# A transposing transfer in place of TensorE transposes in the dot-attention layer of a four-layer graph stack

## The chip, the cores and the metric
The kernel runs on one core of a Trainium2 chip. The metric is the device time of one execution in microseconds (us). Engines are called by the names of the profile: PE (TensorE matmul), PEld (TensorE weight load), DVE (VectorE), ACT (ScalarE), POOL (GpSimd) and SP (SyncE, which here only issues DMAs; SPq is its queue).

## The reference
The input x has shape 16 x 1024 x 64 (16 graphs of 1024 nodes with 64 channels), adj is a 1024 x 1024 mask. Four layers follow one another, each `x = x + layer(relu(layernorm(x)))`. Layers 0 and 3 are additive graph attention, layer 1 is a softmax per channel. The change touches layer 2, which is dot attention:

```
h = jnp.einsum('bnc,hdc->bhnd', x, Wh)            # 4 heads of 64
scores = jnp.einsum('...nd,...md->...nm', h, h)   # masked, softmax over m
out_h = jnp.einsum('...nm,...md->...nd', attn, h) + b
z = leaky_relu(cat(out_h)); h2 = z @ Wo.T         # 256 -> 64
out2 = attention of h2 with itself, as above; then leaky_relu and layernorm
```

So for each graph there are five attentions of 1024 x 1024 scores: four heads, and one over the projected heads, called the out unit.

## The kernel before
**Units.** Layer 2 is a list `UNITS` of 80 units, run one after the other: for each graph b head 0, head 1, the out unit of graph b - 1, head 2, head 3 (the first graph has no out unit between, and the last out unit comes later, inside layer 3). Every engine has its own program with this order written out by hand; semaphores join them.

**A tile.** A unit has T = 8 tiles of 128 rows. Tile jt has these steps: `dots` (PE, L1819: 8 matmuls with 512 columns into one of two score buffers S), the exponential from S to one of eight buffers of `ring` (ACT, L1066), the multiplication by the mask (DVE, L1412, `masked_weights`), and `dot_sums` (PE, L1638: 32 matmuls of 65 columns into ACC). PE issues `dots` of tile m and then `dot_sums` of tile m - LAG, with LAG = 3.

**Features.** The scores need the unit's features with the 64 channels on partitions, as a high fp16 part and the rest, also fp16 ("hi" and "lo"), stacked in FA: FA[:, par, 0] holds hi on partitions 0 to 63 and lo on 64 to 127, FA[:, par, 1] the two swapped. FA has two buffers (par), so features of the next unit are made beside the present one. They are made in this order, with the tile of the present unit in which each step stands in the program of its engine:
- tile 0: PE `values` (L1862), the projection by Wh or Wo, into both banks of AX, 64 columns for each of 8 node tiles; ACT `values` copies it to `v_pairs` (L1086) and squares it (L1087);
- tile 1: DVE `norms` (L1437, L1439) for the bound that the exponential subtracts;
- tile 2: PE `features` (L1871), four 128x128 fp32 transposes of `v_pairs` into AX bank 1; ACT copies the sums of the unit before (L877), then makes hi (L1100); DVE `epilogue` of the unit before (L1420, L1421);
- tile 3: DVE `feature_rest` makes lo (L1429); PE `spread_bound` (L1628); DVE `bias` (L1445) follows in tile 4;
- SP issues four DMAs of 64 KB after hi and four after lo (L513, L514, L519, L520). The first `dots` of the next unit waits for all eight (`features_in`).

POOL adds the bias to the values (L797), which gives V, the right side of `dot_sums`.

**Beside it.** In head 0 and head 3, PE turns two finished heads for the projection by Wo (`turn_heads`, L1839, 8 transposes, both banks of AX); ACT copies them to z_t (L1107). In head 3 this stands in tile 5 on PE and tile 6 on ACT; in head 0 in tile 6. In head 2, PE turns the normalized x of the next graph (`turn_norm`). The banks of AX are handed out by a table (`AX_AT`, filled by `place`), and each user waits until the last one freed its bank; DVE's `bias` frees bank 0.

Of the kernel before, what the change touches and what calls it, by code (L numbers as in the profile page):

```python
# [11 lines left out]
P = 128  # L12
# [18 lines left out]
def gnn_stack(nc, x, adj, w_gat0, w_gat0_t, a_gat0, w0, b0, wa, ba, wh_t, bh, wo_t, bo, gamma, beta,  # L31
# [11 lines left out]
    with ExitStack() as ctx:  # L43
# [79 lines left out]
        hi = sb("hi", [P, 2, HALF], F16)  # L123
        lo = sb("lo", [P, 2, HALF], F16)
        sq = sb("sq", [P, TD])
        v_by_pair = sb("v_pairs", [P, TD])
        v_pairs = v_by_pair[:, :].rearrange("p (q h d) -> p h q d", q=T // 2, h=2)
# [145 lines left out]
        lo_made = sem("lo_made")  # L273
        features_in = [sem("features_in0"), sem("features_in1")]
# [69 lines left out]

        def moved_by(u):

            return 16 * 8 * (u["n"] // 2 + 1)
# [53 lines left out]
        def place_values(u):  # L401

            for half in range(2):
                place(("V", u["n"], half), half)

        def place_features(u):

            place(("F", u["n"]), 1)
# [13 lines left out]
        place_features(UNITS[0])  # L422
        place_bound(UNITS[0])
        for u in UNITS[:-1]:
            if after(u):
                place_values(after(u))
                place_features(after(u))
                place_bound(after(u))
# [20 lines left out]
        place_features(LAST)  # L449
# [45 lines left out]
        def _(sp):  # L495
# [10 lines left out]
            for u in UNITS:  # L506
                par = buf_of(u)
                moved = features_in[par]
                sp.wait_ge(hi_made, u["n"] + 1)
                for half in range(2):  # L510
                    cols_of = slice(half * HALF, (half + 1) * HALF)
                    own = slice(half * D, (half + 1) * D)
                    sp.dma_start(FA[0:D, par, 0, cols_of], hi[own, par, :]).then_inc(moved, 16)  # L513
                    sp.dma_start(FA[D:P, par, 1, cols_of], hi[own, par, :]).then_inc(moved, 16)  # L514
                sp.wait_ge(lo_made, u["n"] + 1)
                for half in range(2):
                    cols_of = slice(half * HALF, (half + 1) * HALF)
                    own = slice(half * D, (half + 1) * D)
                    sp.dma_start(FA[D:P, par, 0, cols_of], lo[own, par, :]).then_inc(moved, 16)  # L519
                    sp.dma_start(FA[0:D, par, 1, cols_of], lo[own, par, :]).then_inc(moved, 16)  # L520
# [9 lines left out]
        def _(pool):  # L530
# [329 lines left out]
        def _(act):  # L860
# [219 lines left out]
            def values(u):  # L1080

                for half in range(2):
                    k, at = AX_AT["V", u["n"], half]
                    act.wait_ge(ax_full[k], at + 1)
                wait(act, v_made, u["n"])
# [5 lines left out]
                for k in range(2):  # L1091
                    act.sem_inc(ax_free[k], 1)

            def features(u):

                k, at = AX_AT["F", u["n"]]
                act.wait_ge(ax_full[k], at + 1)
                if u["n"] >= 2:
                    act.wait_ge(features_in[buf_of(u)], moved_by(UNITS[u["n"] - 2]))
                act.activation(hi[:, buf_of(u), :], AX[k][:, :], ACT.Copy).then_inc(hi_made, 1)  # L1100
# [12 lines left out]
            def dot_unit(u, jt):  # L1113
# [11 lines left out]
                if jt == 6 and is_head(u, 3):  # L1125
# [55 lines left out]
        def _(dve):  # L1181
# [242 lines left out]
            def feature_rest(u):  # L1424

                k, at = AX_AT["F", u["n"]]
# [3 lines left out]
                dve.wait_ge(lo_made, u["n"] + 1)  # L1430
                dve.sem_inc(ax_free[k], 1)
# [60 lines left out]
            def features(u):  # L1492
                norms(u)
                feature_rest(u)
# [12 lines left out]
            def last_layer():  # L1507
# [13 lines left out]
                for jt in range(T):  # L1521
# [56 lines left out]
        def _(pe):  # L1578
# [159 lines left out]
            def last_layer():  # L1738
# [12 lines left out]
                for jt in range(T):  # L1751
# [5 lines left out]
                    if jt == 2:  # L1757
                        features(LAST)
# [83 lines left out]
            def values(u):  # L1842
                n, out_unit = u["n"], u["kind"] == "out"
                if out_unit:
# [5 lines left out]
                chunks = range(2 if out_unit else 1)  # L1850
                for half in range(2):
                    take_bank(AX_AT["V", n, half])
                for t in range(T // 2):
                    for half in range(2):
                        for i in chunks:
                            for c in range(2):
# [3 lines left out]
                                else:  # L1860
                                    rows, w = node_tiles(u["b"], t, half, c), wh[half * D:(half + 1) * D, u["h"], :]
                                last = pe.matmul(AX[half][c * CUT:(c + 1) * CUT, t * D:(t + 1) * D], rows, w,  # L1862
# [99 lines left out]
```

## Time and profile before

| | |
|---|---|
| median of 3 runs | 1996.86 us (1995.81 to 1998.15) |
| the profiled execution | 1996.86 us, span 1995.1 us |
| PE busy | 1904.9 us (95%) |
| DVE busy | 1623.2 us (81%) |
| ACT busy | 1243.6 us (62%) |
| POOL busy | 1013.7 us (51%) |
| units of layer 2 (80) | about 408 us to 1785 us of the span, one more about 1815 us |

A unit begins with its first row of L1819 in the timeline of PE, and the projection (L1862) stands one tile behind that start. The projection tells which unit it is: `AX<-wo,z_t` stands in head 1 (the next unit is the out unit), `AX<-wh,h_t` in the others.

### The profile page before, as it was taken

What the parts mean: (1) busy time and instruction counts of PE and PEld (TensorE: products, weight loads), DVE (VectorE), ACT (ScalarE), POOL (GpSimd) and SP (SyncE); (2) the same over time, 40 slices, a digit from 0 to 9 for tenths busy, and PEclk for the clock granted to TensorE, in tenths of its full rate; (3) what the DMA queues carried; (4) which work ended last, traced back from release to release, by engine and by line L of the source; (5) the groups of instructions that cost most, each with busy time, mean ns of one, the idle gap of its engine ahead of it and who ended that gap; (6) DMA issues with size and microseconds to landing.
All of it is one profiled execution on the core that took longest, in us unless ns stands there. A gap on an engine that the chain in (4) does not pass through costs nothing.

```text
span 1995.1 us, 95063 instructions
## 1 busy us (share of the span) xinstructions
PE 1904.9 (95%) x43624; PEld 1563.2 (78%) x43624; DVE 1623.2 (81%) x1975; ACT 1243.6 (62%) x1886; POOL 1013.7 (51%) x742
## 2 busy tenths in 40 slices
PE   8998899999999999999999999999999999989998
PEld 6787799977777777777777777777777777767887
DVE  6999999567787878778787878788778877767998
ACT  5887676246666666666666666666666666654342
POOL 6676899432345444444544444553445454253653
PEclk7999999999999999999999999999999999999999
DMA  7000000011111111111111111111111111101111
GB/s 182 4 4 4 3 2 3 2 34 35 35 34 34 32 33 33 30 35 34 35 35 32 35 28 35 33 34 35 34 34 29 34 31 33 35 13 25 25 25 35
DMA packets 88255, 61.24 MB, mean 31 GB/s; under 512 B 45616, under 2 KB 86832, under 8 KB 87856
## 3 DMA queue, kind: packets, MB, share of 16 engines
q1 hardware_dynamic: 85632, 54.57, 11.2%
q8 instruction: 343, 5.62, 1.2%
q10 hardware_dynamic: 2224, 0.59, 0.1%
q14 instruction: 56, 0.46, 0.1%
HBM read 8.98 MB, written 4.19 MB: 7 GB/s over the span
## 4 chain that ended last, share of the span: by engine, by line
PE 69%; DVE 15%; ACT 5%; POOL 5%; issue 2%; DMA 2%; SPq 1%; ACTq 0%; POOLq 0%; DVEq 0%
PE ACC L1638 29%; PE S L1819 22%; PE S L1798 8%; DVE ring L1412 6%; PE AX L1862 3%; DVE ring L1266 2%; PE AX L1871 2%; PE AX L1839 2%; POOL sp_log L788 1%; POOL ln_sq L791 1%; DMA FA<-lo 1%; ACT ring L1066 1%; PE AX L1618 1%; DVE score L1421 1%; PE S L1695 1%
## 5 line engine op out<-in xcount | busy, mean ns | idle before, releaser
L1638 PEld LDWEIGHTS ACC<-V,ring 128*64 128x64 f32 x28672 | 953.5, 138 | 180.5 <-DVE ring L1266 34.0
L1412 DVE TENSOR_TENSOR ring<-ring,mask_self_t 128x1024 f32<-128x1024 f32 x640 | 822.1, 1287 | 270.0 <-ACT ring L1066 261.3
L1638 PE MATMUL ACC<-V,ring 128*64 128x65 f32 x28672 | 972.6, 223 | 29.7 <-DVE ring L1266 12.3
L1066 ACT ACTIVATE ring<-S,dot_bias 128x1024 f32<-128x1024 f32 x640 | 713.4, 1115 | 420.3 <-PE S L1819 384.4
L1819 PE MATMUL S<-FA 128*64 128x512 f16 x5120 | 666.5, 382 | 7.5 <-DMA FA<-lo 7.5
L1819 PEld LDWEIGHTS S<-FA 128*64 128x64 f16 x5120 | 253.3, 110 | 168.6 <-ACT ring L1066 15.9
L1266 DVE SCALAR_TENSOR_TENSOR ring<-S,pair_q,mask_t 128x1024 f32<-128x1024 f32 x256 | 315.1, 1272 | 15.1 <-DVE f_max L1278 4.6
L804 POOL TENSOR_TENSOR EV_both<-score,recip 128x512 f32<-128x512 f32 x64 | 115.4, 1803 | 222.3 <-DVE score L1421 222.2
L797 POOL TENSOR_TENSOR V<-v_pairs,bh_bc 128x512 f32<-128x512 f32 x64 | 95.4, 1490 | 164.9 <-ACT v_pairs L1086 164.9
L1798 PE MATMUL S<-parts,mask_t 128*128 128x128 bf16 x3072 | 172.0, 219 | 1.6 <-DVE o L1401 1.4
L1798 PEld LDWEIGHTS S<-parts,mask_t 128*128 128x128 bf16 x3072 | 171.6, 98 | 1.8 <-issue 1.8
L877 ACT ACTIVATE accs<-ACC 128x520 f32<-128x520 f32 x112 | 66.7, 596 | 95.3 <-PE ACC L1638 95.3
L600 POOL TENSOR_TENSOR ln_rstd<-ln_ve,neg_half 128x8 f32<-128x8 f32 x16 | 39.8, 2490 | 87.3 <-DVE ln_ve L1257 87.3
L1086 ACT ACTIVATE v_pairs<-AX 128x512 f32<-128x512 f32 x80 | 47.8, 598 | 55.9 <-PE AX L1862 55.9
L788 POOL TENSOR_TENSOR sp_log<-relu_z,on_mean 128x512 f32<-128x512 f32 x16 | 30.3, 1891 | 93.5 <-DVE on_mean L1455 93.5
L649 POOL TENSOR_TENSOR V<-V 128x512 f32<-128x512 f32 x32 | 33.8, 1055 | 80.7 <-ACT V L937 80.7
L590 POOL TENSOR_TENSOR ln_xc<-X,ln_mean 128x512 f32<-128x512 f32 x16 | 21.5, 1344 | 98.5 <-DVE ln_mean L1249 98.5
L804 POOL TENSOR_TENSOR relu_z<-score,recip 128x512 f32<-128x512 f32 x16 | 32.6, 2039 | 66.8 <-DVE score L1421 66.8
L1399 DVE RECIPROCAL ch_rden<-S 128x512 f32<-128x512 f32 x16 | 53.6, 3350 | 15.4 <-PE S L1798 12.9
L1421 DVE SCALAR_TENSOR_TENSOR score<-accs 128x512 f32<-128x512 f32 x80 | 64.6, 808 | 0.0
L1437 DVE TENSOR_REDUCE norm<-sq 128x8 f32<-128x512 f32 x80 | 54.2, 677 | 8.2 <-ACT sq L1087 8.2
L1839 PE MATMUL AX<-ident,EV_both 128*128 128x128 f32 x256 | 34.5, 278 | 22.8 <-DVE norm_all L1445 22.7
(134 smaller groups left out, 2078.9 us busy)
## 6 DMA issues: line engine op xcount, KB each, us to landing
FA<-hi SPq DMA_DIRECT2D x320, 64.0 KB, 2.0
FA<-lo SPq DMA_DIRECT2D x320, 64.0 KB, 2.0
X<-in_x SPq DMA_DIRECT2D x16, 256.0 KB, 5.0
ring<-in_adj SPq DMA_DIRECT2D x8, 512.0 KB, 8.4
out_x<-X SPq DMA_DIRECT2D x16, 256.0 KB, 2.6
wh<-in_wh_t ACTq DMA_DIRECT2D x2, 64.0 KB, 6.5
bh_bc<-in_bh ACTq DMA_DIRECT2D x1, 128.0 KB, 9.7
w_gat<-in_w_gat ACTq DMA_DIRECT2D x4, 16.0 KB, 3.7
```

What stands on the lines that cost most here:

```text
L797: pool.tensor_tensor(halves_of(V[:, u["n"] % 3, :, 1:D + 1]), v_pairs, halves_of(chans(bias)), ALU.add)\
L804: pool.tensor_tensor(dst, tiles(leaky[:, :]), cols(recip[:, :]), ALU.mult).then_inc(z_epi, 1)
L877: act.activation(accs_4d, acc_all, through).then_inc(acc_copied, 1)
L1066: act.activation(ring[:, jt, :], S[jt % 2][:, :], ACT.Exp, bias=dot_bias[:, n % 2:n % 2 + 1])\
L1266: dve.scalar_tensor_tensor(out=ring[:, jt, :], in0=S[par][:, :], scalar=pair_q[:, par, jt:jt + 1], in1=mask_t[:, jt, :], op0=ALU.max, op1= ...
L1412: dve.tensor_tensor(ring[:, jt, :], ring[:, jt, :], mask_self_t[:, jt, :], ALU.mult)\
L1421: dve.scalar_tensor_tensor(out=tiles(leaky[:, :]), in0=accs[:, :, 0:D], scalar=SLOPE, in1=accs[:, :, 0:D], op0=ALU.mult, op1=ALU.max).then ...
L1638: last = pe.matmul(acc_of(t)[rows, :], ring[:, jt, t * P + c * CUT:t * P + (c + 1) * CUT], values, start=(jt == 0 and t % 4 == 0), stop=(j ...
L1798: last = pe.matmul(S[par][:, t * P:(t + 1) * P], mask_t[:, j, t * P:(t + 1) * P], parts[:, k % 3, part, j, :], start=(j == 0 and part == 0 ...
L1819: last = pe.matmul(S[jt % 2][rows, cut], FA[:, buf, 0, jt * P + c * CUT:jt * P + (c + 1) * CUT], FA[:, buf, i, cut], start=(i == 0), stop= ...
L1839: last = pe.transpose(AX[k][:, t * P:(t + 1) * P], z[:, row, chunk * P:(chunk + 1) * P], ident[:, :])
L1862: last = pe.matmul(AX[half][c * CUT:(c + 1) * CUT, t * D:(t + 1) * D], rows, w, start=(i == 0), stop=(i == chunks[-1]), skip_group_check=True)
```

## The change
The hi and lo parts are made in node layout from a plain copy of the values, without a transpose on PE, into one buffer HL of 128 columns for each node tile (64 of hi, 64 of lo). One transposing DMA brings HL to FA[:, par, 0]; SP waits for it and then issues two DMAs of 128 KB that write the swapped half. Heads 0 and 1, and heads 2 and 3, share one projection with 128 columns, made in the unit before the first of the two (`leads`); the copy of it has 1024 columns. For head 1 and head 3 only the square is left of `values`. In head 3, `turn_heads` moves from tile 5 to tile 7 on PE, and from tile 6 to tile 7 on ACT. The DVE order within a unit stays.

```diff
 # SP
-                sp.wait_ge(hi_made, u["n"] + 1)
-                ... four DMAs of hi, 64 KB each
                 sp.wait_ge(lo_made, u["n"] + 1)
-                ... four DMAs of lo, 64 KB each
+                sp.dma_start_transpose(out=FA[:, par, 0, :].rearrange("p (t n) -> p t n", t=T),
+                                       in_=HL[:, par, :, :].rearrange("p t n -> p (t n)")).then_inc(stacked[par], 16)
+                sp.wait_ge(stacked[par], 16 * (u["n"] // 2 + 1))
+                sp.dma_start(FA[0:D, par, 1, :], FA[D:P, par, 0, :]).then_inc(features_in[par], 16)
+                sp.dma_start(FA[D:P, par, 1, :], FA[0:D, par, 0, :]).then_inc(features_in[par], 16)
 # POOL
-                pool.tensor_tensor(halves_of(V[:, u["n"] % 3, :, 1:D + 1]), v_pairs, halves_of(chans(bias)), ALU.add)\
+                pool.tensor_tensor(V[:, u["n"] % 3, :, 1:D + 1], plain_of(u), chans(bias), ALU.add)\
 # ACT values(u)
-                act.activation(v_pairs, V_FULL, ACT.Copy).then_inc(v_copied, 1)
-                act.activation(sq[:, :].rearrange("p (h n) -> p h n", h=2), AX_both[:, :, 0:T // 2 * D], ACT.Square)\
-                    .then_inc(sq_made, 1)
-                act.wait_ge(sq_made, u["n"] + 1)
+                if leads(u):
+                    ... waits for both banks, v_made and lo_made of the unit before
+                    if u["kind"] == "out":
+                        act.activation(halves_of(plain_of(u)), V_FULL, ACT.Copy).then_inc(v_copied, 1)
+                    else:
+                        act.activation(v_plain[:, :, :, :].rearrange("p t s d -> p (t s d)"),
+                                       AX_both[:, :, :].rearrange("p h n -> p (h n)"), ACT.Copy).then_inc(v_copied, 2)
                 act.wait_ge(v_copied, u["n"] + 1)
+                act.activation(tiles(sq[:, :]), plain_of(u), ACT.Square).then_inc(sq_made, 1)
 # ACT features(u)
-                act.activation(hi[:, buf_of(u), :], AX[k][:, :], ACT.Copy).then_inc(hi_made, 1)
+                act.activation(HL[:, buf_of(u), :, 0:D], plain_of(u), ACT.Copy).then_inc(hi_made, 1)
-                if jt == 6 and is_head(u, 3):
+                if jt == 7 and is_head(u, 3):
                     turned(b, 0)
 # DVE feature_rest(u)
-                dve.tensor_tensor(lo[:, par, :], AX[k][:, :], hi[:, par, :], ALU.subtract).then_inc(lo_made, 1)
+                dve.tensor_tensor(HL[:, par, :, D:2 * D], plain_of(u), HL[:, par, :, 0:D], ALU.subtract)\
+                    .then_inc(lo_made, 1)
 # DVE, the last unit
+                    if jt == 3:
+                        feature_rest(LAST)
                         norms(LAST)
-                    if jt == 5:
-                        feature_rest(LAST)
 # PE values(u): returns at once where the unit doesn't lead
-                                    rows, w = node_tiles(u["b"], t, half, c), wh[half * D:(half + 1) * D, u["h"], :]
+                                    rows = node_tiles(u["b"], t, half, c)
+                                    w = wh[half * D:(half + 1) * D, u["h"]:u["h"] + 2, :].rearrange("p h d -> p (h d)")
-            def features(u):
-                pe.wait_ge(v_copied, u["n"] + 1)
-                k = take_bank(AX_AT["F", u["n"]])
-                for q in range(T // 2):
-                    last = pe.transpose(AX[k][:, q * P:(q + 1) * P], v_by_pair[:, q * P:(q + 1) * P], ident[:, :])
-                last.then_inc(ax_full[k], 1)
-                if jt == 5 and is_head(u, 3):
+                if jt == 7 and is_head(u, 3):
                     turn_heads(b, 0)
```

## Rows read from the trace of the kernel before

**Rows 1.** Page, part 1: busy time, share of the span and instructions of each engine.
```profile
PE 1904.9 (95%) x43624; PEld 1563.2 (78%) x43624; DVE 1623.2 (81%) x1975; ACT 1243.6 (62%) x1886; POOL 1013.7 (51%) x742
```

**Rows 2.** Page, part 4: the chain that ended last, shares of the span by engine.
```profile
PE 69%; DVE 15%; ACT 5%; POOL 5%; issue 2%; DMA 2%; SPq 1%; ACTq 0%; POOLq 0%; DVEq 0%
```

**Rows 3.** Waits of PE, 560 to 1700 us: total us, times, longest us.
```profile
PE AX L1839 <- DVE norm_all L1445: 22.1, 13, 1.7
```

**Rows 4.** Timeline of PE, 1030.5 to 1118 us: start, duration, instructions, [idle before].
```profile
1030.72 1.05 PE L1819 MATMUL S<-FA 128*64 128x512 f16 x8
...
1047.75 1.05 PE L1819 MATMUL S<-FA 128*64 128x512 f16 x8 [0.81 <-DMA FA<-lo]
...
1050.30 1.05 PE L1819 MATMUL S<-FA 128*64 128x512 f16 x8
1052.11 1.03 PE L1819 MATMUL S<-FA 128*64 128x512 f16 x8
...
1054.59 1.05 PE L1819 MATMUL S<-FA 128*64 128x512 f16 x8
...
1056.63 1.03 PE L1819 MATMUL S<-FA 128*64 128x512 f16 x8
1058.43 1.03 PE L1819 MATMUL S<-FA 128*64 128x512 f16 x8
...
1064.52 1.03 PE L1819 MATMUL S<-FA 128*64 128x512 f16 x8
...
1083.44 1.03 PE L1819 MATMUL S<-FA 128*64 128x512 f16 x8
...
1100.62 1.03 PE L1819 MATMUL S<-FA 128*64 128x512 f16 x8
...
1117.77 0.60 PE L1819 MATMUL S<-FA 128*64 128x512 f16 x4
```

**Rows 5.** Timeline of DVE, the same stretch: the lo part, and one mask step.
```profile
1042.02 0.68 DVE L1429 TENSOR_TENSOR lo<-AX,hi 128x512 f16<-128x512 f32 x1
...
1053.00 1.23 DVE L1412 TENSOR_TENSOR ring<-ring,mask_self_t 128x1024 f32<-128x1024 f32 x1 [1.70 <-ACT ring L1066]
...
1058.04 0.68 DVE L1429 TENSOR_TENSOR lo<-AX,hi 128x512 f16<-128x512 f32 x1
...
1076.44 0.68 DVE L1429 TENSOR_TENSOR lo<-AX,hi 128x512 f16<-128x512 f32 x1
...
1093.70 0.69 DVE L1429 TENSOR_TENSOR lo<-AX,hi 128x512 f16<-128x512 f32 x1
...
1112.00 0.68 DVE L1429 TENSOR_TENSOR lo<-AX,hi 128x512 f16<-128x512 f32 x1
```

**Rows 6.** Timeline of ACT, the same stretch, in head 2's unit.
```profile
1050.51 0.60 ACT L1086 ACTIVATE v_pairs<-AX 128x512 f32<-128x512 f32 x1 [0.46 <-PE AX L1862]
...
1051.86 1.11 ACT L1066 ACTIVATE ring<-S,dot_bias 128x1024 f32<-128x1024 f32 x1 [0.27 <-ACT sq L1087]
```

**Rows 7.** Timeline of SP, the same stretch: first and last issue of lo.
```profile
1042.72 0.46 SPq L519 DMA_DIRECT2D FA<-lo  x1
...
1044.52 0.60 SPq L520 DMA_DIRECT2D FA<-lo  x1
```

**Rows 8.** Page, part 6: DMA issues, count, KB each, median us to landing.
```profile
FA<-lo SPq DMA_DIRECT2D x320, 64.0 KB, 2.0
X<-in_x SPq DMA_DIRECT2D x16, 256.0 KB, 5.0
ring<-in_adj SPq DMA_DIRECT2D x8, 512.0 KB, 8.4
out_x<-X SPq DMA_DIRECT2D x16, 256.0 KB, 2.6
```

**Rows 9.** Timeline of PE where layer 3 begins.
```profile
1762.99 1.11 PE L1618 MATMUL AX<-ident,ln_y 128*128 128x128 f32 x4 [5.00 <-POOL ln_y L578]
```

**Rows 10.** Stretch behind it: us; PE, PEld, DVE, ACT, POOL busy; clock; DMA; GB/s.
```profile
1763.00:1767.00 4.00, 4.00 (x38) 2.73 (x40) 0.00 (x0) 1.54 (x2) 2.08 (x2) 0.51 0.00 0
```

More of the change, by code:

```diff
@@ L343, in buf_of, with leads, plain_of @@
             return u["n"] % 2
+        def leads(u):
+            return u["kind"] == "out" or u["h"] % 2 == 0
+        def plain_of(u):
+            return v_plain[:, :, 0 if leads(u) else 1, :]
         def moved_by(u):
-            return 16 * 8 * (u["n"] // 2 + 1)
+            return 16 * 2 * (u["n"] // 2 + 1)
         AX_AT = {}
@@ L401, in place_values @@
         def place_values(u):
[L403 to L408, printed above, removed]
+            if leads(u):
+                for half in range(2):
+                    place(("V", u["n"], half), half)
         def place_bound(u):
@@ L1080, in values @@
             def values(u):
[L1082 to L1085, printed above, removed]
-                act.activation(v_pairs, V_FULL, ACT.Copy).then_inc(v_copied, 1)
-                act.activation(sq[:, :].rearrange("p (h n) -> p h n", h=2), AX_both[:, :, 0:T // 2 * D], ACT.Square)\
-                    .then_inc(sq_made, 1)
-                act.wait_ge(sq_made, u["n"] + 1)
+                if leads(u):
+                    for half in range(2):
+                        k, at = AX_AT["V", u["n"], half]
+                        act.wait_ge(ax_full[k], at + 1)
+                    wait(act, v_made, u["n"])
+                    wait(act, lo_made, u["n"])
+                    if u["kind"] == "out":
[3 more added lines that the diff above has]
+                                       AX_both[:, :, :].rearrange("p h n -> p (h n)"), ACT.Copy).then_inc(v_copied, 2)
                 act.wait_ge(v_copied, u["n"] + 1)
-                for k in range(2):
-                    act.sem_inc(ax_free[k], 1)
+                act.activation(tiles(sq[:, :]), plain_of(u), ACT.Square).then_inc(sq_made, 1)
+                if leads(u):
+                    for k in range(2):
+                        act.sem_inc(ax_free[k], 1)
             def features(u):
-                k, at = AX_AT["F", u["n"]]
-                act.wait_ge(ax_full[k], at + 1)
                 if u["n"] >= 2:
-                    act.wait_ge(features_in[buf_of(u)], moved_by(UNITS[u["n"] - 2]))
-                act.activation(hi[:, buf_of(u), :], AX[k][:, :], ACT.Copy).then_inc(hi_made, 1)
+                    act.wait_ge(stacked[buf_of(u)], 16 * (u["n"] // 2))
+                act.activation(HL[:, buf_of(u), :, 0:D], plain_of(u), ACT.Copy).then_inc(hi_made, 1)
             def turned(b, chunk):
@@ L1492, in features @@
             def features(u):
+                feature_rest(u)
                 norms(u)
-                feature_rest(u)
             def dot_layer():
@@ L1843, in values @@
                 n, out_unit = u["n"], u["kind"] == "out"
+                if not leads(u):
+                    return
                 if out_unit:
@@ L1850, in values @@
                 chunks = range(2 if out_unit else 1)
+                width = D if out_unit else 2 * D
                 for half in range(2):
@@ L1860, in values @@
                                 else:
-                                    rows, w = node_tiles(u["b"], t, half, c), wh[half * D:(half + 1) * D, u["h"], :]
-                                last = pe.matmul(AX[half][c * CUT:(c + 1) * CUT, t * D:(t + 1) * D], rows, w,
+                                    rows = node_tiles(u["b"], t, half, c)
+                                    w = wh[half * D:(half + 1) * D, u["h"]:u["h"] + 2, :].rearrange("p h d -> p (h d)")
+                                last = pe.matmul(AX[half][c * CUT:(c + 1) * CUT, t * width:(t + 1) * width], rows, w,
                                                  start=(i == 0), stop=(i == chunks[-1]), skip_group_check=True)
@@ L1885, in dot_unit @@
                     values(after(u))
-                if jt == LAG - 1 and after(u):
-                    features(after(u))
                 if jt == 3 and after(u):
@@ L1900, in first_features @@
                 values(UNITS[0])
-                features(UNITS[0])
             def dot_layer():
```

27 lines of the change are left out of this document (4 added, 23 removed).

## The prediction
> **What bounds the kernel now.** I read the page first. PE is busy 95% of the span, DVE 81% [rows 1], and the chain that ended last is 69% PE [rows 2], so time on PE counts nearly one to one. Next come the waits in layer 2. PE has one of its own there that is large: 22.1 us in 13 waits of up to 1.7 us, before the turned heads, for the DVE reduction that frees bank 0 [rows 3]. Then I read the timeline of PE over one graph's five units. They begin at 1030.72 (out), 1047.75 (head 2), 1064.52 (head 3), 1083.44 (head 0) and 1100.62 (head 1), and the next out unit at 1117.77: lengths 17.0, 16.8, 18.9, 17.2 and 17.15, in all 87.05 us. Before the second stands an idle 0.81 us for the feature DMAs [rows 4]. That is the row to notice: the transfer of lo is already the late one in the out unit, and the other units aren't far from it.
>
> **What PE does in a unit.** From differences of starts [rows 4]: a tile costs 1.80 (1056.63 to 1058.43), eight 14.35. The bound's spread adds 2.04 - 1.80 = 0.24 (1054.59 to 1056.63), the four transposes 2.48 - 1.80 = 0.68 (1052.11 to 1054.59), the projection 2.55 - 1.80 = 0.75 (1047.75 to 1050.30). Tiles and spread make 14.6. The rest of each length names what else is in it: head 2 16.8 - 14.6 - 0.68 - 0.75 = 0.75 for the turned norm; head 0 17.2 - 16.03 = 1.1 for turned heads; head 3 another 1.75 above that, the wait of rows 3; head 1 17.15 - 15.28 = 1.87 for the projection by Wo.
>
> **What the change takes from PE.** The transposes go: 5 x 0.68 = 3.4 us per graph. Two of four projections go, 1.5. The two that are left have 128 columns: between 0.75 (weight loads set it) and 1.5 (columns set it); I take 1.1, the middle, so +0.7. In head 3 the turned heads stand two tiles later, behind the DVE step that frees the bank, so the 1.75 goes. PE alone would need: head 1 14.6 + 1.87 = 16.5; out 14.6 + 1.1 = 15.7; head 2 14.6 + 0.7 = 15.3; head 3 14.6 + 1.1 + 1.1 = 16.8; head 0 15.7. That is 80.0 us, 7 less per graph, 112 us in 16 graphs, 1885 us. This is the floor, and it is reached only if the features come in time.
>
> **When lo is made.** The DVE order isn't touched, so lo still follows the mask of tile 3. Counted from the start of its unit, lo ends [rows 4, 5] at 1042.70 - 1030.72 = 12.0 (out), 11.0 (head 2), 12.6 (head 3), 10.95 (head 0), 12.05 (head 1). From the mask of tile 1 to the end of lo, head 2 takes 1058.72 - 1053.00 = 5.7 [rows 5], which is DVE back to back: taking transposes from PE doesn't shorten it. What the change moves is the exponential of tile 1 ahead of it. In head 2 it starts at 1051.86, 4.1 behind the unit's start, because ACT first copies and squares the values [rows 6]. In head 2 and head 0 there is no projection and no copy any more; that exponential then waits for its scores only, 1.8 + 1.05 + 0.2 = 3.05, so lo ends at 9.95. In out and head 3 the copy has 1024 columns, 1.11 in place of 0.60 (the exponential of that size is the row), and the projection 0.35 more: lo ends 0.9 later in out, 12.9, and some 0.25 later in head 3, 12.85, where other DVE work already covered part. Head 1 stays, 12.1. The sum of the five is 57.8. The square and hi now read SBUF instead of PSUM; I cost that at nothing, as both stand behind a wait of the same length.
>
> **How long from lo to FA.** Now: four issues from 1042.72, the last at 1044.52 [rows 7], and 2.0 to landing [rows 8], 3.8 in all; with the slow landing of that unit 5.05 (1042.70 to 1047.75). After the change nothing can be issued with hi: it is lo, the transposing DMA (call its time to landing t), SP's wait, an issue of 0.5, and the second swap DMA. That one has 128 KB, between 2.0 (64 KB) and 2.6 (256 KB) [rows 8]; I take 2.2. With 0.15 for two semaphores T = t + 2.85. Two landings stand in a row where one stood. SP has nothing else to do in layer 2, so no other work queues behind its new wait; who waits is the first `dots` of the next unit, and behind it the last three `dot_sums` of the present one, and then ACT and DVE.
>
> **The balance.** A unit takes the longer of its PE work and (end of lo + T). Where all five are set by the features, a graph takes 57.8 + 5T, and it breaks even with 87.05 at T = 5.85, that is t = 3.0 us. Every us beyond costs 5 x 16 = 80 us. So the sign hangs on a DMA of which the trace has no example. Its bounds by rows 8: 2.0 (64 KB on the same queue; nothing with four times the bytes lands sooner) and 8.4 (512 KB in a queue that is full of loads). The nearest rows by bytes are the two of 256 KB, 2.6 and 5.0. The output one is undisturbed like this one, but moves rows of 256 bytes and more unchanged, while this one must re-order single 2-byte elements into 128 partitions. I take the middle of the two, t = 3.8.
>
> The Trainium skill weighs on both sides here. Its page "Advanced Engine Details and Errata", section "X-Bar Transpose (TRN2)", says that transposing DMAs are as fast as ordinary ones; by that t would be the 2.6 of the output row, the first rival. Its page "VectorE: DVE Perf Modes", section "The three transpose paths", gives 1309 ns for one 128x128 block by DMA; eight such blocks one behind the other would be an estimate of 10.5 us, a graph would take 57.8 + 5 x 13.3 = 124 us, and the kernel some 2600 us before any loss of clock: the second rival. No row before shows such a transfer.
>
> **The sum at t = 3.8.** T = 6.65; a graph takes 57.8 + 33.25 = 91.05, 4.0 more than now: 16 x 4.0 = 64 us. The idle before the next unit is end of lo + T less PE's work: head 1 2.25, out 3.85, head 2 1.3, head 3 2.7, head 0 0.9. One more loss follows from that. After an idle of 5.0 us at the start of layer 3 [rows 9] the granted clock was 0.51 for the next 4 us [rows 10], the lower of the two levels (1.2 of 2.4 GHz); the 1.7 us waits of rows 3 are followed by tiles of full speed. Some 1.4 us are lost where it falls (a tile of 3.2 instead of 1.8). I charge it to the out unit alone, whose idle is nearest to 5: 16 x 1.4 = 22 us; its bounds are 0 and, with head 3, 45. Outside these units: the first one's features (0 to +3 us) and the last one's, whose lo is made two tiles earlier (-1 to +2); I put both at 0. Sum: 64 + 22 = +86 us on the profiled execution's 1996.86, which is also the median: 2083, I say 2080.
>
> **Rivals.**
> (a) The transposing transfer is about as quick as a plain one, t of 2.0 to 2.9. At 2.6, T = 5.45: head 1 17.55, out 18.35, head 2 15.4, head 3 18.3, head 0 15.7 (PE again), 85.3 in all, 1.75 less per graph: 1969 us. At 2.0: T = 4.85, 83.4 in all, 1938 us. For it: the 2.6 row, the idle DMA engines in layer 2. Against it: two landings in series, and a window of only 1 us. It ends on the other side; it decides from t under 3.0.
> (b) The transfer goes by small pieces, t of 5 us and more. At the row of 8.4: T = 11.25, 57.8 + 56.25 = 114, idle of 5 to 9 us in every unit and so 1.4 of slow clock in each, 121 in all, 34 more per graph: 2540 us. For it: elements of 2 bytes. Against it: the bytes are few.
> (c) Gain and loss cancel, t of 2.95 to 3.05: 1993 to 2001 us.
> (d) DVE becomes the bound once PE is relieved. Against it: its 81% [rows 1] are some 14.5 of 17.4 us per unit, under PE's 15.3; it sets the end only through lo, as counted. No chance of its own.
>
> **Chances.** The forecast (t from 3.05 to 5) 0.38; (a) 0.36; (b) 0.20; (c) 0.06. A difference of 0.2%, 4 us, is about what a measurement of this kernel can tell from no change. So faster 0.36, same 0.06, slower 0.58. The range takes in (a) almost to its end of 2.0 and goes up to t of about 6 (80 x 3 + 80 us of clock): 1940 to 2320. The likeliest case's own range is 2000 to 2240.
>
> **What would show it.** Right: idle of PE in front of the first `dots` of nearly every unit, released by the swap DMA; the transposing DMA's landing near 3.8 in part 6 of the page; the end of lo at 9.95 behind the start of heads 0 and 2; no row of L1871; the waits of L1839 for `norm_all` gone; projections of 1.1. Wrong: landing under 3 us, or PE starts set by its own work, then (a); landing of 5 and more and a granted clock under 1 across layer 2, then (b). If lo ends elsewhere than counted, the break-even moves by as much.

## The result and the profile after

The changed kernel takes 2127.82 us (2120.79 to 2133.13 in 4 runs), the one before 1996.34 us (1995.45 to 1998.15): a ratio of 1.0655 (95% interval 1.0618 to 1.0692), 131 us slower. The forecast was slower, 2080 us; the range of its likeliest case was 2000 to 2240. So the direction was right and the time lies in the range, but the loss was forecast at 86 us and is 131. The profiled execution took 2133.13 us, 136 more than that of before.

The page of the kernel after, part 1, answers [rows 1]. PE is busy 11 us longer, although 1344 matmuls went (part of it ran at the lower clock, below), and its share fell from 95% to 90%.
```profile
PE 1916.0 (90%) x42280; PEld 1582.4 (74%) x42280; DVE 1689.0 (79%) x1975; ACT 1237.9 (58%) x1854; POOL 1004.8 (47%) x742
```
Part 4, the chain, answers [rows 2]. PE fell from 69% to 33%, DMA rose from 2% to 22%: no engine bounds the kernel now, a loop does, from DVE through two landings to PE and back.
```profile
PE 33%; DVE 26%; DMA 22%; ACT 9%; issue 5%; POOL 3%; SPq 2%; ACTq 0%; POOLq 0%; DVEq 0%
```
Part 6, DMA issues, answers [rows 8]; the last number is the median to landing. The transposing transfer (256 KB) lands in 3.1 us, the swaps in 2.3.
```profile
FA<-FA SPq DMA_DIRECT2D x160, 128.0 KB, 2.3
...
out_x<-X SPq DMA_DIRECT2D x16, 256.0 KB, 2.6
FA<-HL SPq DMA_TRANSPOSE x80, 3.1
```
The waits of PE from 560 to 1800 us (total, times, longest) answer [rows 3]. The wait of the turned heads is gone, 22.1 us. In its place PE waits 128.4 us for the swap (116.1 us up to 1700 us, the window of [rows 3]).
```profile
PE S L1812 <- DMA FA<-FA: 128.4, 66, 3.6
PE AX L1623 <- DVE norm_max L1435: 0.4, 2, 0.3
```
The timeline of PE after, over the starts of one graph's units (head 2 at 1113.86, head 3, head 0, head 1, out), answers [rows 4]. Every unit starts out of an idle for the swap; that holds for all 78 changes from one unit to the next, with idles of 0.38 to 3.63 us (79 of the 80 units stand in a row, the 80th is the one inside layer 3). Behind the longest of the five, the 32 `dot_sums` matmuls take 1.90 us instead of 1.14 and the next `dots` 1.92 instead of 1.03.
```profile
1113.86 1.05 PE L1812 MATMUL S<-FA 128*64 128x512 f16 x8 [3.06 <-DMA FA<-FA]
1114.75 1.90 PE L1633 MATMUL ACC<-V,ring 128*64 128x65 f32 x32
1116.43 1.92 PE L1812 MATMUL S<-FA 128*64 128x512 f16 x8
1118.13 1.14 PE L1633 MATMUL ACC<-V,ring 128*64 128x65 f32 x32
1119.11 1.03 PE L1812 MATMUL S<-FA 128*64 128x512 f16 x8
...
1132.03 1.05 PE L1812 MATMUL S<-FA 128*64 128x512 f16 x8 [0.82 <-DMA FA<-FA]
...
1150.90 1.05 PE L1812 MATMUL S<-FA 128*64 128x512 f16 x8 [1.69 <-DMA FA<-FA]
...
1168.42 1.05 PE L1812 MATMUL S<-FA 128*64 128x512 f16 x8 [1.36 <-DMA FA<-FA]
...
1187.16 1.05 PE L1812 MATMUL S<-FA 128*64 128x512 f16 x8 [1.86 <-DMA FA<-FA]
```
The window behind the first of these starts (us; PE, PEld, DVE, ACT, POOL busy; granted clock; DMA; GB/s), beside the next window of the same unit: 0.66 on average over five microseconds, with the lower of the two levels (1.2 GHz) in most of it. It answers [rows 10].
```profile
1114.00:1119.00 5.00, 5.00 (x78) 3.70 (x76) 1.23 (x1) 2.19 (x3) 0.00 (x0) 0.66 0.00 0
1120.00:1125.00 5.00, 4.99 (x120) 4.08 (x118) 4.97 (x8) 3.85 (x5) 1.50 (x1) 1.00 0.02 5
```
The timeline of DVE after answers [rows 5]: the last mask before lo and lo, in the out unit and in head 3.
```profile
1104.23 1.22 DVE L1409 TENSOR_TENSOR ring<-ring,mask_self_t 128x1024 f32<-128x1024 f32 x1
1105.37 1.53 DVE L1426 TENSOR_TENSOR HL<-v_plain,HL 128x512 f16<-128x512 f32 x1
...
1142.88 1.21 DVE L1409 TENSOR_TENSOR ring<-ring,mask_self_t 128x1024 f32<-128x1024 f32 x1
1144.01 0.68 DVE L1426 TENSOR_TENSOR HL<-v_plain,HL 128x512 f16<-128x512 f32 x1
```
The timeline of POOL after, its division L798 in the same two units:
```profile
1104.39 1.96 POOL L798 TENSOR_TENSOR EV_both<-score,recip 128x512 f32<-128x512 f32 x1 [4.25 <-DVE score L1418]
...
1141.89 1.04 POOL L798 TENSOR_TENSOR EV_both<-score,recip 128x512 f32<-128x512 f32 x1 [4.25 <-DVE score L1418]
```
In head 3, where DVE has other steps between, the division is over (1142.93) before lo begins, and lo takes 0.68, as in all rows of before [rows 5]. In the out unit both overlap. The mask runs to 1105.45 and the division only ends at 1106.35, 0.9 behind it, though it began at 1104.39 and takes 1.04 alone; lo, issued at 1105.37, ends 0.55 after the division. These times fit mask, division and lo taking turns; that they do is inferred from starts and ends. Over the whole trace, 62 of the 80 lo steps overlap a division, and all of them take 1.52 to 1.54; the 18 others take 0.68 to 0.69. Before, 64 of the 80 overlapped a division and all took 0.68 to 0.69: there one input of lo was AX, in PSUM. Before, too, the division itself was stretched beside a mask (1041.04, beside the mask at 1040.88) and short where DVE ran no mask (1074.32, head 3). Timeline of POOL before:
```profile
1041.04 1.96 POOL L804 TENSOR_TENSOR EV_both<-score,recip 128x512 f32<-128x512 f32 x1 [0.63 <-DVE score L1421]
...
1074.32 1.04 POOL L804 TENSOR_TENSOR EV_both<-score,recip 128x512 f32<-128x512 f32 x1 [3.83 <-DVE score L1421]
```

The timeline of SP after answers [rows 7]: one unit's three issues.
```profile
1126.11 1.49 SPq L510 DMA_TRANSPOSE FA<-HL  x1
1129.16 0.46 SPq L513 DMA_DIRECT2D FA<-FA  x1
1129.66 0.60 SPq L514 DMA_DIRECT2D FA<-FA  x1
```
Lo ends at 1126.08, the swaps are issued 3.1 and 3.6 us later, and `dots` starts at 1132.03: T, from the end of lo to the first `dots` of the next unit, is 5.95 here. Over 78 changes of unit the mean of T is 6.56 (5.91 to 7.85): 0.03 to the issue, 3.38 to the first swap (median 3.07), 0.51 to the second, 2.64 to `dots` (median 2.37). The end of lo, counted from the start of its unit, sums to 62.5 us over a graph's five units, by the means (61.4 by the medians).

### The profile page after: what moved, and what is told of

It is laid out like the page before. It is cut to its first block, busy times and chain, and to the rows that moved or that the text cites. A ratio compares the mean times of both kernels' runs of the same rounds, so it can differ in the third digit from the quotient of the medians.

```text
span 2131.2 us, 91704 instructions
## 1 busy us (share of the span) xinstructions
PE 1916.0 (90%) x42280; PEld 1582.4 (74%) x42280; DVE 1689.0 (79%) x1975; ACT 1237.9 (58%) x1854; POOL 1004.8 (47%) x742
## 4 chain that ended last, share of the span: by engine, by line
PE 33%; DVE 26%; DMA 22%; ACT 9%; issue 5%; POOL 3%; SPq 2%; ACTq 0%; POOLq 0%; DVEq 0%
PE ACC L1633 12%; DMA FA<-HL 12%; DVE ring L1409 12%; DMA FA<-FA 9%; PE S L1812 8%; PE S L1791 7%; DVE HL L1426 5%; ACT ring L1060 4%; PE AX L1859 3%; DVE ring L1263 2%; DVE norm L1433 2%; SPq L513 2%; DVE score L1418 2%; ACT v_plain L1085 2%; ACT st_x L899 1%
## 5 line engine op out<-in xcount | busy, mean ns | idle before, releaser
L1409 DVE TENSOR_TENSOR ring<-ring,mask_self_t 128x1024 f32<-128x1024 f32 x640 | 861.0, 1355 | 351.2 <-ACT ring L1060 350.1
L1633 PEld LDWEIGHTS ACC<-V,ring 128*64 128x64 f32 x28672 | 991.4, 141 | 194.6 <-issue 76.1
L1633 PE MATMUL ACC<-V,ring 128*64 128x65 f32 x28672 | 1010.3, 226 | 31.1 <-DVE ring L1263 12.3
L1812 PE MATMUL S<-FA 128*64 128x512 f16 x5120 | 695.4, 392 | 156.8 <-DMA FA<-FA 153.8
L1812 PEld LDWEIGHTS S<-FA 128*64 128x64 f16 x5120 | 285.7, 113 | 305.9 <-DMA FA<-FA 166.1
L798 POOL TENSOR_TENSOR EV_both<-score,recip 128x512 f32<-128x512 f32 x64 | 112.1, 1752 | 272.1 <-DVE score L1418 272.0
L791 POOL TENSOR_TENSOR V<-v_plain,bh_bc 128x512 f32<-128x512 f32 x64 | 97.4, 1521 | 78.4 <-ACT v_plain L1085 78.4
L798 POOL TENSOR_TENSOR relu_z<-score,recip 128x512 f32<-128x512 f32 x16 | 29.6, 1850 | 219.3 <-DVE score L1418 219.3
L1426 DVE TENSOR_TENSOR HL<-v_plain,HL 128x512 f16<-128x512 f32 x80 | 107.3, 1341 | 10.5 <-ACT HL L1097 10.5
L584 POOL TENSOR_TENSOR ln_xc<-X,ln_mean 128x512 f32<-128x512 f32 x16 | 21.5, 1344 | 96.5 <-DVE ln_mean L1246 96.5
L1085 ACT ACTIVATE v_plain<-AX 128x1024 f32<-128x1024 f32 x32 | 32.7, 1023 | 42.7 <-PE AX L1859 42.7
L1418 DVE SCALAR_TENSOR_TENSOR score<-accs 128x512 f32<-128x512 f32 x80 | 51.6, 645 | 0.0
```

The lines of the kernel that those rows point to most:

```text
L791: pool.tensor_tensor(V[:, u["n"] % 3, :, 1:D + 1], plain_of(u), chans(bias), ALU.add)\
L798: pool.tensor_tensor(dst, tiles(leaky[:, :]), cols(recip[:, :]), ALU.mult).then_inc(z_epi, 1)
L1085: act.activation(v_plain[:, :, :, :].rearrange("p t s d -> p (t s d)"), AX_both[:, :, :].rearrange("p h n -> p (h n)"), ACT.Copy).then_inc ...
L1409: dve.tensor_tensor(ring[:, jt, :], ring[:, jt, :], mask_self_t[:, jt, :], ALU.mult)\
L1418: dve.scalar_tensor_tensor(out=tiles(leaky[:, :]), in0=accs[:, :, 0:D], scalar=SLOPE, in1=accs[:, :, 0:D], op0=ALU.mult, op1=ALU.max).then ...
L1426: dve.tensor_tensor(HL[:, par, :, D:2 * D], plain_of(u), HL[:, par, :, 0:D], ALU.subtract)\
```

## The experiments

Each graph's five units are compared by the mean distance of their starts, the very first unit left out: 86.3 us before, 95.2 after. "After" and "before" in a title say which kernel is edited. Ratios are to the kernel before on the same chip.

**1. After, without the overlap of lo and the division.** POOL waits for lo before it divides.
```diff
 # POOL, dot_layer
                 if 0 < u["n"] < LAST["n"]:
+                    if after(u):
+                        pool.wait_ge(lo_made, u["n"] + 2)
                     divide(UNITS[u["n"] - 1])
```


> The changed kernel, with one wait added: POOL's division of the unit before waits until the lo part of the next unit is made. In the changed kernel the lo subtraction takes 1.53 us where POOL's division runs beside it and 0.68 us where it doesn't (head 3). Theory (the lo part is on the path of every unit, and its slowing by POOL is part of the loss): it falls back to 0.68 us, 0.85 us less in four of five units, so 62 x 0.85 = 53 us less than the changed kernel's 2128: about 2075. Rival (the slow subtraction is hidden, the landings and the clock alone set the loss): unchanged, 2120 to 2133.

It took 2055.15 us (2047.91 to 2060.71), 1.0293 (1.0265 to 1.032). Lines by form of this kernel (busy, mean ns), and PE's waits, 560 to 1700 us:
```profile
L1428 DVE TENSOR_TENSOR HL<-v_plain,HL 128x512 f16<-128x512 f32 x80 | 54.7, 683 | 10.5 <-ACT HL L1099 10.5
```
```profile
PE S L1814 <- DMA FA<-FA: 86.2, 54, 3.6
```
Lo is back to 683 ns, and 73 us went, more than half of the whole loss. Four units a graph give 4 x 0.85 x 16 = 54 us. The rest fits the clock: the idles are shorter, and this trace has 13 stretches at the lower level in its row of units where after has 31 (mean granted clock 0.984 for 0.966). The expectation named the right cause and a gain that was too small, since it left out the clock.

**2. Before, with two landings in series, plain DMAs.** Hi and lo go into FA[:, par, 0] only, and the swap follows, as in the change.
```diff
 # SP: of each pair of DMAs of hi and of lo, the one into FA[.., par, 0, ..] stays, on `stacked`
+                sp.wait_ge(stacked[par], 16 * 4 * (u["n"] // 2 + 1))
+                sp.dma_start(FA[0:D, par, 1, :], FA[D:P, par, 0, :]).then_inc(moved, 16)
+                sp.dma_start(FA[D:P, par, 1, :], FA[0:D, par, 0, :]).then_inc(moved, 16)
```


> The kernel before, its features by plain DMAs, but with the second landing of the change: four DMAs write FA[:, par, 0], SP waits for them, two DMAs of 128 KB write the swapped half. Theory (a unit takes the longer of PE's work and end of lo plus transfer): the transfer takes 5.4 us at its median and 6.2 at its mean, against 5.1 in head 1 and 4.1 to 4.8 in out that are free; between 1 and 3 us per graph, 2015 to 2045. Rival (waiting for one landing before the next issue is by itself what costs the 131 us): 2090 or more.

2054.11 us (2049.07 to 2058.76), 1.0289 (1.0267 to 1.0311). The waits of PE:
```profile
PE S L1821 <- DMA FA<-FA: 40.8, 37, 2.6
PE AX L1841 <- DVE norm_all L1447: 16.2, 13, 1.7
```
The second landing costs 58 us by itself, with no transposing transfer in the kernel. The mean distance from the end of lo to the next unit was 4.6 (out) to 6.3 us (head 3) before, where PE's own work sets it in most units; here it is 6.15 to 6.44 in all five. The measured time lies between the expectation (2015 to 2045) and its rival (2090 or more): the expectation set the cost too low.

**3. After, two transposing DMAs and no swap.** HL has a second copy with hi and lo the other way round, made by one more ACT and one more DVE step, and one DMA for each.
```diff
-                sp.wait_ge(stacked[par], 16 * (u["n"] // 2 + 1))
-                ... the two swap DMAs
+                sp.wait_ge(hi2_made, u["n"] + 1)
+                sp.wait_ge(lo2_made, u["n"] + 1)
+                sp.dma_start_transpose(out=FA[:, par, 1, :]..., in_=HL[:, par, 1, :, :]...)
 # ACT
+                act.activation(HL[:, buf_of(u), 1, :, D:2 * D], plain_of(u), ACT.Copy).then_inc(hi2_made, 1)
 # DVE
+                dve.tensor_copy(HL[:, par, 1, :, 0:D], HL[:, par, 0, :, D:2 * D]).then_inc(lo2_made, 1)
```


> The changed kernel, with the second landing taken away: HL is kept in both orders (hi|lo and lo|hi; ACT writes hi twice, DVE copies lo once), and two transposing DMAs are issued one behind the other where the changed kernel waits for one and then issues two swap DMAs. Theory (end of lo plus transfer sets the unit; a large part of the transfer is that second landing): the transfer falls from 6.8 us to the issue of the first (1.23) plus the landing of the second (3.1 to 3.4), 4.5 to 4.9; lo ends up to 0.3 later; three units still wait for it, two reach PE's own time: some 84 to 86 us per graph against 95.2, 1955 to 1990. Rival (two transposes behind each other take each other's time, so nothing is won by dropping the swap): the second lands 6 us or more behind lo, 2080 or more.

2000.89 us (1994.61 to 2003.72, 10 runs), 1.0014 (1.0004 to 1.0024). The timeline of SP and the row of part 6:
```profile
1093.62 1.23 SPq L512 DMA_TRANSPOSE FA<-HL  x1
1094.95 1.28 SPq L516 DMA_TRANSPOSE FA<-HL  x1
```
```profile
FA<-HL SPq DMA_TRANSPOSE x160, 3.2
```
Two transposing DMAs 1.33 us apart land in 3.2 each (medians; the means are 3.6), so the second doesn't pay for the first. 127 us of the loss go, but not all through the second landing. The mean of T falls from 6.56 to 5.2, some 107 us in 80 units; the end of lo falls by 1.7 us a graph, another 28 us, because only 29 lo steps of this kernel overlap a division and not 62, and because there are fewer drops of the clock. The expected 1955 to 1990 was missed: T was expected at 4.5 to 4.9, and its parts are, by the means, 1.47 us to the second issue, 3.6 to its landing and 0.09 to `dots`.
```profile
PE S L1820 <- issue: 44.4, 43, 2.3
PE S L1820 <- DMA FA<-HL: 7.6, 5, 2.0
```
The larger of these waits carries no name ("issue"), but the trace says what it is: in 68 of the 78 changes of unit, and in all 63 with an idle of PE, `dots` starts 0.09 us behind the landing of the second transposing DMA. PE still waits for the transfer here, some 61 us in all.

**4. Before, with the turned heads of head 3 in tile 7**, and nothing else of the change.
```diff
-                if jt == 5 and is_head(u, 3):
+                if jt == 7 and is_head(u, 3):
                     turn_heads(b, 0)
```
(and the same for ACT's `turned`, from 6 to 7.)


> The kernel before, with one part of the change alone: in head 3 the two finished heads are turned in tile 7 (PE, ACT) instead of 5 and 6. Theory: the wait of 1.7 us for the DVE reduction goes in 15 units, 25 us less: 1970 to 1975. Rival (the features' transfer is next and takes its place): 1985 to 1997.

1977.25 us (1974.0 to 1980.14), 0.9904 (0.9888 to 0.992). Head 3 went from 18.74 to 17.37 us, the wait for `norm_all` is gone. This part of the change is worth 18 to 19 us. The expectation (1970 to 1975) had counted the full 1.7 us in each graph.

**5. After, features two tiles earlier.** ACT makes hi in tile 0 (in after: tile 2), DVE lo in tile 1, ahead of the norms (in after: tile 3).
```diff
 # ACT
                 if jt == 0 and after(u):
                     values(after(u))
+                    features(after(u))
-                if jt == LAG - 1 and after(u):
-                    features(after(u))
 # DVE
                 if jt == 1 and nxt:
+                    feature_rest(nxt)
                     norms(nxt)
-                if jt == 3 and nxt:
-                    feature_rest(nxt)
```


> The changed kernel with hi made in tile 0 (ACT, right behind the square) and lo in tile 1 (DVE, ahead of the norms), two tiles earlier; all else as it is. Theory (only the lateness of the features costs time): the end of lo moves from 11 to 13 us behind the unit's start to about 6.5 (heads 0 and 2) and 8.5 (the others); with 6.8 us to FA it is at hand before PE has done its work (15.3 to 16.8 us), so PE sets the units again, near the floor of 80 us per graph: 1885 to 1915, faster than both kernels. First rival (DVE becomes the bound when PE is relieved): 1930 to 1980. Second rival (the transfers themselves disturb, or the clock stays low): above 2000.

1952.82 us (1948.86 to 1954.48), 0.9776 (0.9758 to 0.9793): 175 us under the change as it was, and faster than before. The waits of PE, 560 to 1700 us:
```profile
PE ACC L1631 <- issue: 12.2, 27, 0.5
PE AX L1621 <- DVE norm_max L1434: 12.1, 14, 1.5
PE S L1810 <- DMA FA<-FA: 1.6, 3, 0.7
```
Lo now ends 6.25 to 9.1 us behind a unit's start, outside the division (in the out unit it still takes 1.53, beside other work of POOL), and T (8.3 to 9.7) is no longer what the transfer takes but has slack in it. The same two landings that cost 116 us of idle in this window now cost 1.6. The expected 1885 to 1915, the floor, was missed: a graph takes 83.65 us, not 80.0. The time lies in the range of the first rival, a DVE that becomes the bound, and DVE is 87% busy (1700.9 us). But that cause isn't shown, and experiment 8 speaks against it: there, steps change their place, DVE is busy as long (1698.7 us), and 19 us go.

**6. Experiment 5 without the shared projection**, each head projecting its own 64 columns:
```diff
 # leads(u)
-            return u["kind"] == "out" or u["h"] % 2 == 0
+            return True
```
(with a copy of 512 columns in each unit, and a projection `width` of D.)


> The version with hi and lo made early (1953 us), with the projections as before the change: one of 64 columns for each unit, in place of one of 128 columns for two. In that version the features are in time, so the worth of the shared projection shows by itself. Theory (PE's work counts): four projections of 0.75 us in place of two of 1.04, 0.9 us per graph more, 1967. Rival (in the units that make a shared projection, ACT's copy of 1024 columns holds up the exponential of tile 1 and with it PE, so sharing gives nothing): 1953 or less.

1977.38 us (1976.14 to 1978.61), 0.9896 (0.9881 to 0.991). Sharing is worth 25 us, where the features aren't late; neither the expected 1967 nor the rival's 1953 came. PE's own saving was forecast as 2 x 0.75 - 0.7 = 0.8 us per graph, 13 us. The rest fits DVE, though no run parts it: lo takes 996 ns on average for 840 in experiment 5, and PE's wait for `norm_max` is longer, 33.5 us in 38 times against 12.1 in 14:
```profile
PE AX L1620 <- DVE norm_max L1433: 33.5, 38, 1.5
```

**7. After, with filler matmuls** where PE would stand idle: 16 of the form of `dots`, into the score buffer that is overwritten next. They add no result. The wait for `features_in` moves behind the one for the score buffer.
```diff
 # PE, before the wait for features_in
+                    if 0 < n < LAST["n"]:
+                        for k in range(16):
+                            pe.matmul(S[0][...], FA[:, 1 - buf, 0, 0:CUT], FA[:, 1 - buf, 0, 0:HALF], ...)
                     pe.wait_ge(features_in[buf], moved_by(UNITS[n]))
```


> The changed kernel, with 16 matmuls of 512 columns added on PE in front of its wait for the features, in all units but the first and the last; they write S[0], which the scores overwrite afterwards, so nothing of the result changes. They take 1.75 us at full clock, less than the idle time in front of nearly every unit (medians 1.8 to 3.8 us). In the changed kernel's trace 29 stretches of 3.4 us of layer 2 have the lower clock, where the kernel before has one. Theory (the clock falls behind the longer idle times and costs 1 to 1.5 us each time): the low stretches mostly go, 25 to 45 us less than 2128: 2085 to 2105. Rival (what the low clock slows is hidden by the wait for the next features): 2120 to 2135; where the added work isn't hidden, more.

2093.26 us (2092.4 to 2096.37), 1.0485 (1.0469 to 1.0501), and a mean granted clock of 0.993 for 0.966. The timeline of PE of this kernel shows a filler block and the idle that is left:
```profile
1095.03 1.93 PE L1808 MATMUL S<-FA 128*64 128x512 f16 x16
1098.17 1.05 PE L1816 MATMUL S<-FA 128*64 128x512 f16 x8 [1.22 <-DMA FA<-FA]
1099.06 1.10 PE L1633 MATMUL ACC<-V,ring 128*64 128x65 f32 x32
```
With more work on PE, the kernel ends 35 us sooner, as expected. Its trace has no lower level between the first unit and layer 3, where after has 30 stretches. The end of lo falls from 62.5 to 59.7 us a graph while T stays (6.65), so the clock costs its time through lo: `dots`, exponential and mask of the first tiles stand ahead of it. The fillers delay some starts (1.93 us each, where in after 41 of the 78 idles were shorter), so the drops cost at least 35 us.

**8. A version from these.** To experiment 5: `spread_bound` from tile 3 to 4 (PE), `bias` from tile 4 to 5 (DVE), and the turned heads of head 0 from tile 6 to 7 (PE, ACT), so that each stands behind what it waited for. A first version also moved the norms to tile 2 and the square behind the sums of tile 2; the diff shows what both have in common.
```diff
 # PE and ACT: turn_heads, turned
-                if jt == 6 and is_head(u, 0) and b > 0:
+                if jt == 7 and is_head(u, 0) and b > 0:
 # PE
-                if jt == 3 and after(u):
+                if jt == 4 and after(u):
                     spread_bound(after(u))
 # DVE
-                if jt == 4 and nxt:
+                if jt == 5 and nxt:
                     bias(nxt)
```


> The version with hi and lo made early (1953 us, 83.65 us per graph where PE's own work is 80), relieved where PE still waits there: ACT's square stands behind the copy of the sums (tile 2) instead of ahead of the exponential of tile 1, DVE's norms stand behind the epilogue of tile 2, the spread on PE moves to tile 4, the bias on DVE to tile 5, and head 0's turned heads to tile 7 like head 3's. Theory (PE waits in the out unit and head 3 for the copy of the sums and for the norms, both late because ACT has three things to do before the exponential of tile 1): 81 to 82 us per graph, 1915 to 1930. Rival (DVE, 87% busy, is the bound by then): 1945 to 1960.

1967.57 us (1966.28 to 1969.98), 0.9851 (0.9834 to 0.9867): 15 us slower than experiment 5, a miss. Its waits and one of its lo steps, on the timeline of DVE:
```profile
PE AX L1628 <- DVE norm_max L1440: 28.2, 25, 1.9
```
```profile
1069.30 1.77 DVE L1431 TENSOR_TENSOR HL<-v_plain,HL 128x512 f16<-128x512 f32 x1
```
PE's wait for `norm_max` grew from 12.1 us to 28.2, and lo met POOL again: 27 of its 80 steps take 1.77. With the moves of norms and square taken back:

> The version with hi and lo made early (1953 us), where only the bound's spread moves from tile 3 to 4 on PE, DVE's bias from tile 4 to 5, and head 0's turned heads from tile 6 to 7 on PE and ACT; square and norms stay in tiles 0 and 1. Theory (the 14 waits for the norms' maximum, 12 to 14 us between 560 and 1700, are real losses of PE, and the version that also moved the norms made them worse, 28 us): 0.9 us per graph less, 1935 to 1945. Rival (the stretch is bound by DVE, and a wait taken away there comes back at the next mask): 1950 to 1956.

1933.71 us (1932.22 to 1935.52), 0.9681 (0.9665 to 0.9697): the fastest of all, 3.2% under the kernel before, and a little better than expected (1935 to 1945). The waits for `norm_max` are gone. Its page, parts 1 and 4:
```profile
PE 1856.3 (96%) x42280; PEld 1550.9 (80%) x42280; DVE 1698.7 (88%) x1975; ACT 1235.9 (64%) x1854; POOL 1037.3 (54%) x742
...
PE 84%; DVE 5%; ACT 4%; POOL 3%; issue 2%; DMA 1%; ACTq 0%; POOLq 0%; SPq 0%; DVEq 0%
```
PE is the chain again, and a graph takes 82.3 us against the floor of 80.0. The rival, a DVE that is the bound (1950 to 1956), is out.

**9. The same, with POOL's bias add waiting for lo**, to keep it from the mask and from lo.
```diff
 # POOL
                 pool.wait_ge(v_copied, u["n"] + 1)
+                pool.wait_ge(lo_made, u["n"] + 1)
```


> The same, and POOL's bias addition to the values waits until lo is made, so that it doesn't run beside the lo subtraction and the masks ahead of it. Theory (POOL work beside DVE's stretches it, 1.5 to 2.1 us for a mask step of 1.2, in the tiles where DVE is the late one): another 5 to 15 us less than the version without it. Rival (POOL's work only moves to other mask steps and slows those): within 4 us of it.

1940.96 us (1940.26 to 1942.01), 0.972 (0.9706 to 0.9734): 7 us slower, outside both the expectation and its rival. DVE's busy time rose from 1698.7 to 1722.8 us, which fits POOL's work meeting other masks instead. The same kind of wait gained 73 us in experiment 1, where lo set the start of every unit, and loses 7 here, where it doesn't.

## Why the prediction came out as it did

The forecast's case happened: T over 5.85 and every unit set by its features. Experiment 5 shows it: make lo early, with the same DMAs, and the idle goes from 116.1 to 1.6 us and the kernel is faster than before. Step by step:

- **PE's floor, 80.0 us a graph: close.** The best version, with PE 96% busy, takes 82.3. The 128-column projections take 1.10 us (1.1 forecast), the waits before the turned heads are gone, and that shift alone is worth 18 to 19 us in experiment 4 (1.75 x 16 = 28 from the one unit of [rows 4]; the mean gain of head 3 is 1.37).
- **Landing t, 3.8 us: too long.** The median is 3.05, the mean 3.36. The row of 2.6 was nearer than the middle taken. By the median, t stands on the border of case (c), "gain and loss cancel"; the clear loss came from the late landings and the swap, and then from lo and the clock. The swap was too short, 2.2 against 2.37 (median) and 2.64 (mean) from issue to `dots`; the 0.15 for two semaphores has no row, and the one that shows, from the end of lo to the issue, is 0.03. That T is 6.56 for 6.65 is luck: the errors cancel. Against the Trainium skill: "Advanced Engine Details and Errata", section "X-Bar Transpose (TRN2)", says as fast as an ordinary DMA; here 3.1 stands against 2.6 for the same 256 KB [rows 8], near, but on the other side of the break-even. The estimate of 10.5 us, eight times the 1309 ns per block of "VectorE: DVE Perf Modes", section "The three transpose paths" in the Trainium skill, is refuted.
- **End of lo, 57.8 us a graph: the step that was mis-sized.** It was 62.5. The prediction said of the square and hi, which now read SBUF, "I cost that at nothing", and said nothing of lo, both inputs of which now lie in SBUF too. Lo takes 1.53 us instead of 0.68 in four of five units, where the division runs beside it: 3.4 us a graph. Experiment 1, which takes that overlap away, shows 73 us for it, with the drops of the clock that go too. The rule was to be had: the Trainium skill, "SBUF — State Buffer", section "Who interferes with whom", says that a DVE instruction with two inputs in SBUF contends with a GpSimd instruction that reads SBUF, and one with at most one input there doesn't (outside the two-port modes). Both halves agree with this case: all 64 overlaps with a division before, with one input in PSUM, left lo at 0.68, and all 62 after made it 1.53. One overlap doesn't follow it: 13 lo steps of head 3 ran beside POOL's L834, which works on 128x8, and stayed at 0.68. The row that could have warned stood in the trace too: POOL's division takes 1.96 beside a mask and 1.04 without (1041.04 and 1074.32, shown above). Without the overlap, lo ended at 56.5 us a graph (medians of experiment 1), 1.3 earlier than forecast, so the rest of this step erred to the careful side.
- **Clock, 22 us: the price was right, the count too small.** In its row of 79 units the trace after has 31 stretches at the lower level, 28 of 3.4 us and three of 6.8, the one where layer 3 begins left out. The one at the first unit stands in before too, which has no other there. The other 30 stand at starts of units. In these units lo ends later than in the others of the same kind: 12.16 against 10.84 (head 0), 14.24 against 12.63 (head 1), 14.04 against 12.83 (out), 12.31 against 10.68 (head 2), 14.04 against 12.64 (head 3). So a drop costs 1.2 to 1.6 us, where 1.4 was forecast, and 30 of them some 44 us, an estimate from these differences; the filler run gives at least 35, both inside the bounds of 0 to 45. The place charged, the idle between the out unit and head 2, has 12 of them and not 16, but 18 others stand at the starts of the other four (out 5, head 3 5, head 0 5, head 1 3). The length of the idle didn't decide alone: drops followed idles of 1.91 to 3.63 us, and nine others of 2.1 to 3.4 us had none.
- **Rival (a), a quick transfer**, failed by little in t (3.05 for its 2.0 to 2.9) and by the rest of T: with the median of each part of T (0.03, 3.07, 0.50, 2.37) and lo at 57.8, a graph takes 57.8 + 5 x 5.97 = 87.65, about the 87.05 of its break-even; with the mean T of 6.56 it takes 90.6. The kernel of experiment 1, with lo at 57.2 by the mean and T at 6.5 to 6.7, took 90.05.
- **Rival (b)**, small pieces, is out: no landing over 4.8 us. **Rival (d)**, a DVE bound, had "no chance of its own", rightly: PE is the one that waits for the swap here, and even at 88% busy DVE wasn't the bound (experiment 8). Its 14.5 of 17.4 us doesn't follow from 81%, which gives 14.1; nothing hangs on it.

The sum again: a graph took 95.2 us where the forecast had 91.05 and 1.4 of clock, 92.45. The end of lo adds 4.65, T takes off 0.5 (32.75 for 33.25), and the 1.4 is taken off, as the loss of clock lies within the measured end of lo: 2.75. Of the 62.5 us to lo, 56.5 are lo without overlap and drops, 3.4 the overlap, and the 2.6 left the clock. The five units before are 86.3 by the mean of all graphs, not the 87.05 of the one graph read, another 0.75. So 3.5 x 16 = 56 us; 6 less outside these units make the profiled execution's 136 out of 86.

## What to carry to other kernels

When an operand of a DVE step moves from PSUM to SBUF, look at what GpSimd does beside it before you price that at nothing. Replacing compute on the bound engine by a DMA lengthens the latency of a chain, so move the chain's source forward in the same edit: here the same DMAs were 6.6% slower with lo in tile 3 and, with lo in tile 1 and the bound steps a tile later, 3.2% faster. When a break-even lies inside the range of one unknown, count all landings in series and use their mean, not the median: where every unit waits for its transfer, the late landings are paid in full, and here T is 5.97 by the medians of its parts and 6.56 by the mean. And ask whether a lost clock falls on the chain that sets the time: here it did, and cost some 1.4 us each time.

## What the runs showed of the hardware

- A transposing DMA of 256 KB from SBUF to SBUF (8 blocks of 128x128 fp16) holds its queue 1.23 us at issue, against 0.46 to 0.60 for a plain one of 128 KB, and lands in 3.0 to 4.8 us, median 3.1. A second one 1.33 us behind lands in 3.2 (median, experiment 3).
- Where a transfer of code into the instruction buffers overlapped, the time from the transposing DMA's issue to the first swap was 3.51 us by the mean (56 cases) and without 3.06 (22 cases, none over 3.10); from the second swap to `dots` it was 3.00 (34) and 2.36 (44). That is a correlation in one trace, not tried by a run. It would explain why the mean of T is above the sum of the medians of its parts.
- A DVE subtraction of 128x512 with both inputs in SBUF took 1.53 us in all 62 overlaps with a POOL division of 128x512, and 0.68 alone or beside POOL's 128x8 step; with one input in PSUM it took 0.68 in all 64 such overlaps (traces after and before).
- A kernel that gives PE 16 useless matmuls per unit is 35 us faster than without (experiment 7).
